# One slot of a software pipeline: gray image, second transposes, state products, edge filter and states' output moved up, in a new order of maxima, projections and drain

## The reference

```python
h = _L0_tok_ref(x, scharr)                 # gray image, 2 edge filters (3x3), sum of magnitudes / 2
h = concatenate([h, _L0_txt_ref(x_txt, U, s, Vt)], axis=1)     # 256 image rows and 128 text rows
h = h + _L0_attn_ref(_layernorm(h), ...)   # 16 heads of 16, local window of 128 keys, softmax
h = h + _L0_ffn_ref(_layernorm(h), ...)    # router keeps 288 of 384 rows; one 256x256 product, gelu
h = h + _L1_attn_ref(_layernorm(h), ...)   # state space layer: a circulant step, done with eigenvalues
h = h + _L1_ffn_ref(_layernorm(h), ...)    # shared expert (1024 wide) and the best 2 of 8 experts
```

## Time and profile before

| | us |
|---|---|
| median of 3 executions | 2193.5 |
| lowest and highest | 2188.15 and 2195.46 |
| the profiled execution, its own time | 2192.07 |
| its span (first to last instruction) | 2190.3 |
| its mean granted TensorE clock | 0.969 |

### The profile page before, as it was taken

How to read it: one execution, slowest core, us unless ns; L and a number is a source line. 1 busy time by engine, 2 the same in 40 slices (tenths; PEclk the granted TensorE clock), 3 DMA queues, 4 the chain that set the end, 5 groups by cost and what they waited for, 6 DMA issues and landing times.

```text
span 2190.3 us, 44925 instructions
## 1 busy us (share of the span) xinstructions
PE 1965.9 (90%) x13651; PEld 1559.6 (71%) x13652; DVE 1350.6 (62%) x3572; ACT 1079.5 (49%) x2513; POOL 819.2 (37%) x1535
## 2 busy tenths in 40 slices
PE   2879999999999999999999999985789999999997
PEld 1546666666666666666666666653689999999997
DVE  5647668577576685775766757643455565555654
ACT  0336455455554554555545555541355455555553
POOL 3113324334243233342432333322344545454454
PEclk8789999999999999999999999996899999999998
DMA  4220211211202112112021121110333232323322
GB/s 138 65 58 9 66 45 29 65 35 45 65 15 65 44 28 65 33 47 65 15 65 43 30 65 31 35 59 8 111 84 84 44 83 47 81 48 81 48 47 40
DMA packets 81090, 116.53 MB, mean 53 GB/s; under 512 B 20965, under 2 KB 61509, under 8 KB 78725
## 3 DMA queue, kind: packets, MB, share of 16 engines
q1 hardware_dynamic: 54948, 85.34, 14.1%
q0 software_dynamic: 23360, 27.91, 7.8%
q10 hardware_dynamic: 2736, 2.76, 0.4%
HBM read 51.58 MB, written 26.71 MB: 36 GB/s over the span
## 4 chain that ended last, share of the span: by engine, by line
PE 51%; DVE 16%; issue 14%; POOL 8%; DMA 5%; ACT 4%; POOLq 0%; DVEq 0%; SPq 0%; ACTq 0%
PE ps L1780 10%; PE ps L1616 8%; POOL slot_rows L658 4%; PE ps L1493 4%; PE ps L1792 3%; PE ps L1791 3%; PE ps L1793 3%; DVE mx L1119 2%; PE ps L1582 2%; PE ps L1465 2%; DMA result<-yb,idx_o 2%; PE ps L1607 2%; PE ps L1561 2%; PE ps L1548 2%; DMA slot_rows<-pay,row_i 2%
## 5 line engine op out<-in xcount | busy, mean ns | idle before, releaser
L793 ACT ACTIVATE prob<-ps,mx 128x256 f32<-128x256 f32 (+1 forms) x768 | 295.0, 443 | 254.9 <-DVE mx L1119 240.1
L897 ACT ACTIVATE hid_hi<-ps,b 128x256 fp32r<-128x256 f32 x408 | 205.8, 504 | 286.1 <-PE ps L1780 286.1
L1119 DVE TENSOR_REDUCE mx<-ps 128x2 f32<-128x512 f32 (+1 forms) x384 | 224.5, 594 | 116.0 <-PE ps L1540 107.3
L785 ACT ACTIVATE pT<-ps 128x512 f32<-128x512 f32 (+1 forms) x384 | 205.2, 534 | 123.9 <-PE ps L1548 120.5
L1395 DVE TENSOR_TENSOR hid_lo<-hid_full,hid_hi 128x256 fp32r<-128x256 f32 x408 | 172.3, 426 | 150.7 <-ACT hid_full L900 150.1
L1539 PE MATMUL ps<-ks,qs 96*128 96x512 f32 (+1 forms) x384 | 186.7, 487 | 63.9 <-ACT prob L793 51.0
L1791 PE MATMUL ps<-w_hi,hid_hi 128*128 128x256 f32 x816 | 232.3, 285 | 0.0
L1792 PE MATMUL ps<-w_lo,hid_hi 128*128 128x256 f32 x816 | 227.9, 279 | 0.0
L1793 PE MATMUL ps<-w_hi,hid_lo 128*128 128x256 f32 x816 | 227.9, 279 | 0.0
L900 ACT ACTIVATE hid_full<-ps,b 128x256 f32<-128x256 f32 x408 | 206.2, 505 | 0.0
L1548 PE MATMUL ps<-ident,prob 128*128 128x128 f32 x1280 | 204.8, 277 | 0.0
(11 more groups left out here) (269 smaller groups left out, 4175.6 us busy)
## 6 DMA issues: line engine op xcount, KB each, us to landing
w_raw<-in_w SPq DMA_DIRECT2D x16, 1024.0 KB, 6.0
xin<-in_x SPq DMA_DIRECT2D x32, 384.0 KB, 3.6
qs<-q_hi SPq DMA_DIRECT2D x128, 96.0 KB, 2.1
ks<-k_hi SPq DMA_DIRECT2D x256, 48.0 KB, 2.1
qs<-q_lo SPq DMA_DIRECT2D x64, 96.0 KB, 2.1
ks<-k_lo SPq DMA_DIRECT2D x128, 48.0 KB, 2.1
xn_rows<-xc SPq DMA_DIRECT2D x16, 384.0 KB, 2.5
result<-h SPq DMA_DIRECT2D x16, 384.0 KB, 2.5
```

The lines of the kernel that those rows point to most:

```text
L785: act.activation(pT[:, u % TB, :, k0:2, :], ps[:, 2 + u % 2, :].rearrange("p (h k q) -> p h k q", h=2, k=2)[:, :, k0:2, :], ACT.Copy).then ...
L793: ins = act.activation(prob[:, s % PB, hh, w], ps[:, s % 2, hh * 2 * P + w.start:(hh + 1) * 2 * P], ACT.Exp, bias=mx[:, s % 2, hh:hh + 1])
L897: act.activation(hid_hi[:, f], ps[:, f % 4, 0:CHUNK], ACT.Gelu_apprx_tanh, bias=b1[half][:, f:f + 1])
L1119: dve.tensor_reduce(mx[:, s % 2], sc, AX_X, ALU.max, negate=True).then_inc(max_done.sem, 1)
```

## The change

Slots: the gray image goes from slot 11 to 10, the second transposes from 12 to 11 (the scaling ahead of them from 11 to 10), the state projection from 14 to 13, the state products from 14 to 13 and on, the filter from 15 to 14 and on, the states' output from 19 to 18, the rows of the next image from 19 to 18. Order within a slot: DVE takes the maximum ahead of the chain in slots 13, 19 and 20, and the third statistics are one slot behind the residual sum; PE has the state projection behind the unit of its slot, the output projection ahead of the value products, the queries ahead of unit 26, one third of the values' sum in slot 1, and in the first transposes waits for hidden block 6 before the first half of them and for block 7 before the second. The drain: POOL's dispatch stands behind the states in the passes without attention; ranks and gate ratio of image 15 stand behind the first hidden block in pass 16; the last shared sum stands behind the fourth of the eight table copies, and PE waits for it before it transposes the first gathered rows.

```diff
-TEXT, GRAY_AT, TURN1 = 3, 11, 12
+TEXT, GRAY_AT, TURN1 = 3, 10, 11
-STATE, CONV, OUT = 14, 15, 19
-ROWS, TURN2, UP, LOGIT = 19, 27, 28, 30
+STATE, CONV, OUT = 13, 14, 18
+ROWS, TURN2, UP, LOGIT = 18, 27, 28, 30
+LATER = (STATE, OUT + 1, OUT + 2)
...
             def sequence(b, att, late, chain, head):
-                if late:
+                if late and att:
                     dispatch(b - 2)
                 if chain:
                     chain_deviations(b - 1, 1)
                     direct_term(b - 1)
                     states(b - 1)
+                if late and not att:
+                    dispatch(b - 2)
...
+                    if first_weights and s == min(UPS):
+                        gate_ratio(b - 1)
                     for f in UPS.get(s, ()) if chain else ():
                         hidden_layer(b - 1, f)
...
             sequence(NB, False, True, True, False, first_weights=True)
-            gate_ratio(NB - 1)
...
                     dve.wait_ge(h3_ready.sem, h3_ready.at(b, 1))
+                if s == OUT + 2:
                     chain_rows(b, 2)
...
-                    if chained:
+                    if chained and s not in LATER:
                         chain(b - 1, s)
                     if att and s == 2:
                         values_sum(b)
                     if att:
                         unit(b, s)
+                    if chained and s in LATER:
+                        chain(b - 1, s)
...
-            shared_sum(NB - 1)
             dve.wait_ge(route_loaded.sem, route_loaded.at(0, 16))
             for e in range(NE):
...
+                if e == 3:
+                    shared_sum(NB - 1)
...
-            def values_sum(b):
+            def values_sum(b, first, last):
...
-                for i in range(NT):
+                for i in range(first, last):
...
-                ins.then_inc(sumv_done.sem, 1)
+                if last == NT:
+                    ins.then_inc(sumv_done.sem, 1)
...
+                if s in WO:
+                    i = WO.index(s)
+                    pe.wait_ge(cxT_ready.sem, cxT_ready.at(b, i + 1))
+                    for k in range(KB):
+                        ins = pe.matmul(ps[:, 5, D:2 * D], cxT[:, k], wo[:, k], start=(k == 0), stop=(k == KB - 1))
+                    ins.then_inc(wo_done.sem, 1)
                 if PV <= s < NU + PV and (s - PV) % 2 == 1:
...
-                if s in WO:
...
-            def turn_chain(b, n, head):
-
+            def turn_chain(b, n, head, first=False):
+
+                if n == 0 and not first:
+                    pe.wait_ge(hid_ready.sem, hid_ready.at(b - 1, FB - 1))
                 pe.wait_ge(xc_ready.sem, xc_ready.at(b, n + 1))
                 pe.wait_ge(xcT_ready.sem, xcT_ready.at(b, n))
-                if n == 0:
-                    pe.wait_ge(hid_ready.sem, hid_ready.at(b, 0))
...
                 for k in range(KB):
+                    if n == 0 and k == 1:
+                        pe.wait_ge(hid_ready.sem, hid_ready.at(b, 0))
...
-                if s == TURN1 + 2:
+            def drive(b):
+
                     pe.wait_ge(xcT_ready.sem, xcT_ready.at(b, 2))
...
+                    if head and s == TURN2 - 1:
+                        queries(b + 1)
                     if att and s == BLOCK:
-                        values_sum(b)
+                        values_sum(b, 1, NT)
...
                     if att:
                         unit(b, s)
+                    if att and s == TURN0:
+                        values_sum(b, 0, 1)
...
+                    if chained and s == TURN1 + 2:
+                        drive(b - 1)
                     if chained and s == OUT:
                         state_out(b - 1, head)
                     if head and s == ROWS + 3:
                         turn_rows(b + 1)
-                    if head and s == TURN2 - 1:
-                        queries(b + 1)
...
+                    if last and s == min(UPS):
+                        slot_ranks(b - 1, False)
...
-            sequence(NB, False, True, True, False)
-            slot_ranks(NB - 1, False)
+            sequence(NB, False, True, True, False, last=True)
...
+            pe.wait_ge(h4_ready.sem, h4_ready.at(NB, 0))
             turn_chunk(0)
```

More of the change, by code:

```diff
@@ L1687, in logits, with sequence @@
                     ins.then_inc(logit_done.sem, 1)
-            def sequence(b, att, late, chained, head, first=False):
+            def sequence(b, att, late, chained, head, first=False, last=False):
                 for s in range(SLOTS):
-                    if first and s == 1:
+                    if first and not chained and s == 1:
                         pe.wait_ge(mats_read.sem, mats_read.at(0, 1))
@@ L1703, in sequence @@
                     if chained and s == TURN0:
-                        turn_chain(b - 1, 0, head)
+                        turn_chain(b - 1, 0, head, first)
                     if att:
                         unit(b, s)
+                    if att and s == TURN0:
+                        values_sum(b, 0, 1)
                     if late and s == RANKS:
@@ L1746, in _ @@
             pe.wait_ge(late_loaded.sem, late_loaded.at(0, NLATE))
-            sequence(1, True, False, True, True)
+            sequence(1, True, False, True, True, first=True)
             with pe.Fori(2, NB - 1) as b:
```

## The result

The changed kernel takes 2236.65 us (2234.05 to 2241.49), the kernel before in the same comparison 2192.47 us; the ratio is 1.0206, with a 95% interval of 1.0181 to 1.0231. That is 44 us more, about 2%.

The account below looks back on a forecast made before the run. PE, 90% busy, was taken to bound the kernel, with 5.7 us of waits a steady pass. Waits +32, clock +12 and last passes -12.3 made +31.7 us, forecasting 2225 us, range 2188 to 2245.

Parts of the forecast that it names:

- The image: Second transposes and scores 13: waits of 1.68 and 3.84 us replace 0.66 and 1.09, adding 3.8 us a pass.
- Filter: PE before the first filter step, behind DVE's rotations: a new wait of 0.5 us in place of 0.2.
- rows' transposes: PE before transposing the text and image rows, whose normalisation comes late: a new wait of 0.9 us.
- start of the pass: First transposes wait for hidden block 6, not 7: 0.3 us gained, nothing more at the router product.
- the four waits named as going: PE waits of 1.06, 0.61, 0.76 and 0.2 us, at unit 22's scores, two value products and elsewhere, subtracted as going.
- The named waits: All PE waits of a steady pass: 3.8 less 1.2 less 0.3, so 2.3 us more a pass.
- The clock: PE's granted clock halves behind the new long wait: between nothing and 24 us over 14 passes, half taken, 12 us.
- My likeliest story: The clock falls in some passes: 2225 us in all, chance 0.42.
- clock falls in every pass: Rival: the long wait costs 1.7 us of clock in each of 14 passes; +44, 2237 us, chance 0.20.
- The last passes: Drain before the experts: earlier routing of image 15 and shared sum start the experts 12.3 us sooner.
- POOL's detour: POOL's dispatch of pass 14 behind the states: second rstd 3.4 us sooner, 1.1 given back, net 2.3.
- Passes 0 and 15: Pass 0 shifts image and filter alike; pass 15's 1 us longer transpose wait is about given back: both at 0.

Follow-up runs that it names:

- image_back: Changed kernel with the gray image alone put back behind unit 11 (slot 11); 2170.21 us, ratio 0.9887 to the kernel before.
- projection_first: Changed kernel with the state projection ahead of unit 13 instead of behind it, image still in slot 10; 2187.15 us, ratio 0.9982 to the kernel before.
- slots_only: Kernel before with the moved slots alone, its order and drain kept, so the projection stands ahead of unit 13; 2214.09 us, ratio 1.0110.
- order_only: Changed kernel with all slots as before the change and its new order kept; 2243.31 us, ratio 1.0226 to the kernel before.
- filled: Changed kernel with 22 unused identity transposes on PE ahead of scores 13 in passes with image and chain; 2205.72 us, ratio 1.0052 to the kernel before.
- order_covered: Changed kernel with the old slots, rotations ahead of the maximum in their slot and the projection ahead of its unit; 2183.12 us, ratio 0.9961 to the kernel before.
- drain_only: Kernel before with the drain's changes alone (dispatch, ranks, gate ratio, last shared sum), passes 0 to 15 untouched; 2180.73 us, ratio 0.9935.
- late_dispatch: Changed kernel with the image back behind unit 11 and POOL's dispatch behind the second rstd and direct term; 2157.08 us, ratio 0.9844 to the kernel before.

## Why the prediction was right, and which step was mis-sized

**The image.** I had the 1.68 us before the transposes, the new wait before scores 13 and the place of maximum 11 from the order alone. Measured: 1.71, and 0.55 with 3.06 for my 3.84. image_back, projection_first, slots_only and order_only tell the parts: it needs both the image ahead of unit 11's maximum (or 12's, in the old slots) and the projection behind the waiting unit. The 0.55 that I had put inside the 3.84 belongs to the transposes' slot: it stands in every kernel with the transposes in slot 11.

**The other steps of a pass.** Filter: 0.20 for my 0.5; rows' transposes 1.33 for 0.9; start of the pass 0.67 gained for 0.3, of which 0.44 at the router product, where I had said that nothing would be earned; the four waits named as going went. The named waits go from 5.5 to 7.3 us, +1.8 where the sum had +2.3.

**The clock** is the mis-sized term. I took one fall in every second pass at 1.7 us, 12 us in all. There was one in every pass from 1 to 14, and from pass 4 on it lasted 6.8 us in place of 3.4 (in pass 2 there were two of 3.4). A pass grew by 4.4 us, of which 1.8 are waits, so some 2.5 us are the clock; filled shows the same 2.5, and 31 us in all. With 31 in place of 12 the sum would have been 2244, and with the waits as measured (14 x 0.5 less) 2237. (14 passes at 2.5 are 35 us; that fits the profiled execution, 2241.5, which took 5 us more than the median.)

My likeliest story, a fall in some passes, did not come true. The measured 2237 lies 12 us above my 2225 and in my range because that reached up past a fall in each pass. The rival "clock falls in every pass", to which I gave 0.20, had the time, 2237, but by the price of a 3.4 us fall and waits that were 0.5 too large: two errors that cancel. The page I named there (the Trainium skill, "TensorE: Matmul & The Clock Gate", section "HAM oscillation") tells of a loop in which a recurring wait put the array on the slow clock at every step. The trace agrees, with a fall in each of 14 passes. But the page's waits are of some 3 to 5 us, and here a fall came behind 1.85 us too (order_covered, 11 of 13 passes).

**The last passes.** 12.1 us between trace marks for my 12.3, and drain_only gave it alone. Inside it the second half of POOL's detour was mis-sized: the third normalisation came 1.5 us sooner, not 2.3. The first DMA of the moved dispatch took 2.87 us beside DVE's subtraction of 3.08, its successors 0.97; drain_only shows 2.87 beside 3.07 and 0.97. I had charged nothing there. (My 1504.0 for the end of the dispatch is also 0.3 over its own terms: 1494.8 and 8.9 make 1503.7.) By the Trainium skill ("SBUF — State Buffer", section "Who interferes with whom") a DVE instruction with two inputs in SBUF contends with a GpSimd instruction that reads SBUF. These rows agree if issuing such a DMA, whose offsets `row_i` lie in SBUF, counts as one. The same section infers that such a DVE instruction doesn't hold up the making of a DMA's descriptors; the 2.87 us speak against that for this indirect DMA. In the kernel before, where that subtraction doesn't lie beside it, the same DMA took 1.12 us.

**Passes 0 and 15**, taken at 0. Pass 15 is at +1.0 by the table; PE waits 2.31 us before its second transposes, and at the end of that wait the clock fell to 0.50 for 3.4 us:

```profile
1465.78 1.11 PE L1613 MATMUL ps<-ident,xc 128*128 128x128 f32 x4 [2.31 <-DVE xc L1040]
```

The start is at +5.5, but pass 1 is in it, with 4.4 of the sum. The rest is within what the start varies by: it is 1.2 longer in drain_only, which leaves passes 0 and 1 as they were.

## What to carry to other kernels

When long work on one engine is hidden by queued work on another, count which instructions of the hiding engine still stand ahead of the first one that needs the result. Moving the long work up by a slot (image_back against the kernel after), or one product of the cover behind that unit (projection_first against it), turns hidden time into waiting, and a total of busy shares shows nothing of it. Price a new TensorE wait in a loop with the slower clock behind it as well: one of 3.06 and one of 3.67 us brought it in every steady pass, one of 1.85 in most passes of one kernel and in none of another. Where the wait can't be removed, useless transposes in it can be cheaper than the clock (2206 us for 2237).

## What was not expected of the hardware

**Short waits can be followed by a fall of the clock.** Behind a wait of 1.85 us in each pass (order_covered) the clock was at half for 3.4 us in 11 of 13, at one of 3.06 with 0.55 before it for 6.8 us in each from pass 4 on (after). Waits of 1.67 and 1.34 (projection_first, late_dispatch) did so in no steady pass, and neither did the 1.85 of order_only. So the length of a wait doesn't tell by itself; what else decides stays open.

**The image's length depends on what POOL does beside it.** The same five DVE instructions took 5.46 us in the earlier trace rows and 4.49 in image_back. There one of them took 2.19 us beside POOL's sum of hc, and the others 0.43 to 0.69. In the kernel before, the first took 0.57 in place of 0.43, and the next three are these, on DVE; below them POOL's sum of hc there and in image_back:

```profile
880.95 1.10 DVE L1046 SCALAR_TENSOR_TENSOR xin<-xin 128x512 f32<-128x512 f32 x1
882.09 1.11 DVE L1048 SCALAR_TENSOR_TENSOR xin<-xin 128x512 f32<-128x512 f32 x1
883.23 1.92 DVE L1050 CAST gray_hi<-xin 128x512 fp32r<-128x512 f32 x1
```

```profile
882.73 2.14 POOL L641 TENSOR_TENSOR hc<-hc,g 128x768 f32<-128x768 f32 x1
877.77 1.88 POOL L642 TENSOR_TENSOR hc<-hc,g 128x768 f32<-128x768 f32 x1
```

Against the start of that sum the image began 2.4 us ahead in the kernel before and 0.2 ahead in image_back. This was worth 1 us, which I had not foreseen, and is most of why image_back has no wait left at the image. No run tried the image without POOL's work beside it, so the cause is read from the overlap alone.
